# Sharing batch 3's expert sums between VectorE and GpSimd, and reordering the work around them, in an eight-layer transformer kernel

## The chip, the cores and the metric

The kernel runs on one core of a Trainium2 chip. The metric is the device time of one execution in microseconds (us). Engines are named as in the profile: PE is TensorE (PEld its weight loads), DVE VectorE, ACT ScalarE, POOL GpSimd, SP the engine that issues most transfers.

## The reference

The input x is 4 batches of 512 rows of 128 floats. Eight layers follow each other, four pairs of a cross-attention over 32 context rows and a feed-forward layer, each added to x after a layer norm:

```python
x = x + _L1_ffn_ref(_layernorm(x, axis=-1), ...)     # 16 experts, the best 3 of each row
x = x + _L2_xattn_ref(_layernorm(x, axis=-1), ...)   # 16 heads, softmax, causal mask

raw_gate = softmax(einsum('btd,de->bte', x, gate))
_, topk_idx = top_k(raw_gate, 3)                     # gates of the three, divided by their sum
hidden = relu(einsum('btd,edh->bteh', x, W1) + b1)
expert_out = einsum('bteh,ehd->bted', hidden, W2) + b2
return einsum('bte,bted->btd', gate_topk, expert_out)
```

The kernel numbers the layers 0 to 7. Layer 3 is the expert layer above, layer 4 the attention behind it. The change lies where layer 3 ends and layer 4 begins.

## The kernel before

x stays in on-chip memory as 16 tiles of 128 rows by 128 columns (tile t belongs to batch t // 4; W = 4 tiles of a batch, T = 16, S = 512, K = TOPK[3] = 3, D = P = 128). Each engine runs a list written out by hand and waits on semaphores. There is no scheduler.

Layer 3 scatters each row to the lists of its three experts in device memory. It then works through 63 slots of 128 rows: SP loads a slot, PE turns it (L2265), does the hidden product (L2273) and the second product (L2286, s_my), ACT does the relu (L1748), DVE adds the bias (L1321), and the rows are stored again. GpSimd gathers the finished rows back with indirect transfers (`gather`, L676, each one 128 rows): 12 for each batch, tile by tile and the three choices of a tile behind each other, three in flight. The first gather of a batch waits for the stores of its last slots (`PRIOR`); for batch 3 that is the last of the 63.

The three gathered rows of a row are weighted with gk and added to x. For batches 0 to 2 DVE does it (`add_experts`, L1308, 12 instructions a batch, four for each choice k). For batch 3 GpSimd does it (`add_last`): one product over all 12 tiles (L687) and three sums (L690). When a batch is summed, DVE takes its statistics (`stats_of`: L846, L849, L851, semaphore s_var), GpSimd the power of the variance (`power`: L630, L635, L637, s_rstd), ACT normalises the batch (`normed`, L1654), PE turns it (L2115, s_xT) and ACT copies the turned batch out of PSUM (`turned`, L1662). `power(n)` waits for the n-th statistics; powers 16 to 19 are those of batches 0 to 3 in layer 4, in this order.

Layer 4 runs in periods, one for each of the 16 tiles: PE computes the scores of tile t (L2127, s_s), DVE takes the maximum over each head and subtracts it (`max_sub`: L1252, L1256, and for the first tile of each batch the causal cap L1242), ACT takes the exponential, PE turns it (L2132) and multiplies with the values (L2143), DVE divides (`normalise`: L1265, L1269). `period(4, t)` of DVE holds `max_sub` of tile t + 1. Batches 1, 2 and 3 are normalised on ACT in its periods 0, 4 and 8 (`LATE`). In DVE's period 7 stands the wait for batch 3's sums (s_sum) and its statistics; until they are done DVE takes no further maximum. `add_bo` (L695) adds a bias to x on GpSimd after a batch was normalised.

Before the change DVE ends the expert layer with the last third of batch 1's sums and its statistics, and then starts period(4, -1), whose only work is the maximum of tile 0.

## Time and profile before

| | |
|---|---|
| median of 3 runs | 573.29 us (572.55 to 574.57) |
| the profiled execution's own time | 575.11 us |
| its span, first to last instruction | 573.4 us |
| granted PE clock, mean | 0.790 of full speed |
| busy share PE / PEld / DVE / ACT / POOL | 75% / 62% / 58% / 42% / 41% |

A row of the profile's timeline gives start and duration in us, engine, line, operation, output from input, and in brackets how long the engine sat idle before it and what ended that. The layer 3 to 4 boundary lies at 355 to 415 us of the span.

### The profile page before, as it was taken

What the parts mean: (1) busy time and instruction counts of PE and PEld (TensorE: products, weight loads), DVE (VectorE), ACT (ScalarE), POOL (GpSimd) and SP (SyncE); (2) the same over time, 40 slices, a digit from 0 to 9 for tenths busy, and PEclk for the clock granted to TensorE, in tenths of its full rate; (3) what the DMA queues carried; (4) which work ended last, traced back from release to release, by engine and by line L of the source; (5) the groups of instructions that cost most, each with busy time, mean ns of one, the idle gap of its engine ahead of it and who ended that gap; (6) DMA issues with size and microseconds to landing.
All of it is one profiled execution on the core that took longest, in us unless ns stands there. A gap on an engine that the chain in (4) does not pass through costs nothing.

```text
span 573.4 us, 9996 instructions
## 1 busy us (share of the span) xinstructions
PE 428.6 (75%) x2628; PEld 355.2 (62%) x2628; DVE 333.1 (58%) x1130; ACT 238.8 (42%) x635; POOL 234.8 (41%) x294
## 2 busy tenths in 40 slices
PE   5879678997898876529984749568899999982550
PEld 4768667995677775219973738436676667771440
DVE  6665355656786436215531317277776767858887
ACT  2332224664544212126752426334565646562221
POOL 2513730036327573720454341747811334533214
PEclk9795568999988557559995859778899999995555
DMA  6999546882651110212442323211000000000002
GB/s 188 299 403 388 122 123 212 290 284 54 203 187 46 34 48 16 80 37 70 130 117 61 98 60 89 74 32 39 0 1 2 1 0 1 2 1 1 0 1 73
DMA packets 60548, 55.42 MB, mean 97 GB/s; under 512 B 11922, under 2 KB 46446, under 8 KB 60366
## 3 DMA queue, kind: packets, MB, share of 16 engines
q1 hardware_dynamic: 53214, 43.64, 23.7%
q0 software_dynamic: 4736, 9.71, 5.8%
q10 hardware_dynamic: 2544, 1.44, 0.8%
q8 instruction: 23, 0.38, 0.3%
q14 instruction: 31, 0.25, 0.1%
HBM read 24.10 MB, written 30.67 MB: 96 GB/s over the span
## 4 chain that ended last, share of the span: by engine, by line
PE 44%; DVE 19%; another core or an unknown queue 9%; issue 9%; ACT 6%; POOL 5%; DVEq 5%; DMA 2%; SPq 2%; ACTq 0%; POOLq 0%
PE bank L2286 9%; PE bank L2273 8%; PE bank L2143 4%; PE bank L2127 3%; PE bank L2265 3%; PE bank L2132 2%; PE bank L2158 2%; PE bank L1982 2%; POOL wall L676 2%; DVE stats L846 2%; ACT xn L1654 2%; DVE e_sb L1256 1%; PE bank L2115 1%; PE bank L2416 1%
## 5 line engine op out<-in xcount | busy, mean ns | idle before, releaser
L1748 ACT ACTIVATE r<-bank,b 128x128 f32<-128x128 f32 x218 | 65.8, 365 | 56.1 <-PE bank L2273 33.8
L630 POOL TENSOR_TENSOR rstd<-veps,mhalf 128x4 f32<-128x4 f32 x32 | 33.8, 1056 | 132.0 <-DVE veps L851 131.6
L2286 PE MATMUL bank<-wall,r 128*128 x436 | 71.6, 299 | 20.9 <-ACT r L1748 17.6
L2286 PEld LDWEIGHTS bank<-wall,r 128*128 128x128 f32 x436 | 60.9, 207 | 23.9 <-issue 23.0
L2273 PE MATMUL bank<-on,e_sb 128*128 128x128 f32 x348 | 61.0, 310 | 9.0 <-issue 6.1
L676 POOL DMA_INDIRECT vZ<-outbuf,slots x40 | 39.2, 979 | 67.5 <-DMA outbuf<-h_sb 49.2
L1321 DVE TENSOR_TENSOR h_sb<-bank,b2all 128x128 f32<-128x128 f32 x86 | 25.0, 290 | 66.6 <-PE bank L2286 47.5
L2273 PEld LDWEIGHTS bank<-on,e_sb 128*128 128x128 f32 x348 | 51.5, 216 | 10.8 <-issue 10.8
L649 POOL DMA_INDIRECT outbuf<-h_sb,slots x48 | 46.5, 970 | 23.0 <-issue 15.1
L2143 PEld LDWEIGHTS bank<-vB,eT 128*128 128x128 f32 x384 | 52.7, 213 | 0.0
L2143 PE MATMUL bank<-vB,eT 128*128 128x36 f32 x384 | 52.5, 287 | 0.0
L1678 ACT COPY eT<-bank 128x512 f32<-128x512 f32 x48 | 28.0, 584 | 43.8 <-PE bank L2132 36.8
L1327 DVE COPY e_sb<-wall 128x256 f32 (+1 forms) x75 | 24.0, 323 | 36.4 <-PE bank L2273 23.2
L2265 PE MATMUL bank<-ident,h_sb 128*128 128x128 f32 x86 | 27.0, 316 | 20.3 <-issue 17.3
L1740 ACT COPY on<-bank 128x128 f32<-128x128 f32 x86 | 22.9, 267 | 44.4 <-PE bank L2265 22.8
L2127 PE MATMUL bank<-aB,xnT_all 128*128 128x512 f32 x64 | 36.0, 650 | 4.9 <-DVE e_sb L1256 4.0
L2132 PEld LDWEIGHTS bank<-ident,e_sb 128*128 128x128 f32 x192 | 25.9, 156 | 21.5 <-ACT e_sb L1674 9.9
L2132 PE MATMUL bank<-ident,e_sb 128*128 128x128 f32 x192 | 32.7, 298 | 2.4 <-ACT e_sb L1674 2.0
L846 DVE BATCH_NORM_STATS2 stats<-x 128x6 f32<-128x128 f32 x128 | 28.0, 281 | 5.3 <-POOL x L690 2.4
L2265 PEld LDWEIGHTS bank<-ident,h_sb 128*128 128x128 f32 x86 | 13.2, 154 | 26.7 <-issue 21.9
L2127 PE MATMUL bank<-VW,xnT_all 128*128 128x512 f32 x32 | 21.1, 752 | 8.5 <-ACT xnT_all L1662 5.0
L1654 ACT ACTIVATE xn<-x,nmr,rstd 128x128 f32<-128x128 f32 x48 | 19.7, 483 | 12.3 <-POOL nmr L637 12.3
(306 smaller groups left out, 876.3 us busy)
## 6 DMA issues: line engine op xcount, KB each, us to landing
outbuf<-zero SPq DMA_DIRECT2D x17, 1024.0 KB
wall<-in_w SPq DMA_DIRECT2D x4, 2048.0 KB, 13.8
outbuf<-h_sb SPq DMA_DIRECT2D x66, 64.0 KB
h_sb<-outbuf SPq DMA_DIRECT2D x63, 64.0 KB
h_sb<-rowbuf SPq DMA_DIRECT2D x23, 64.0 KB
outbuf<-h_sb POOLq DMA_DIRECT2D x20, 64.0 KB, 2.0
x<-in_x ACTq DMA_DIRECT2D x4, 256.0 KB, 6.3
b2all<-in_L_ffn_b SPq DMA_DIRECT2D x1, 1024.0 KB, 15.5
```

Source lines behind the costliest of these rows:

```text
L630: r = nc.gpsimd.tensor_tensor(rstd[:, at], veps[:, at], mhalf[:, 0:W], ALU.pow)
L649: i = nc.gpsimd.indirect_dma_start(rows_of[l][0:MOE[l][0] * REGION * P], bass.IndirectOffsetOnAxis(slots[:, k * T + t:k * T + t + 1], 0), ...
L676: nc.gpsimd.indirect_dma_start(tile_of(yg[l][b], w * K + k), None, outbuf[0:MOE[l][0] * REGION * P], bass.IndirectOffsetOnAxis(slots[:, c: ...
L846: v.bn_stats(stats[:, w * 6:w * 6 + 6], src(w))
L1654: i = a.activation(tile_of(dst, w), tile_of(x, b * W + w), ACT.Identity, bias=nmr[:, c:c + 1], scale=rstd[:, c:c + 1])
L1748: i = a.activation(hT[:, u * 512 + c * P:u * 512 + (c + 1) * P], bank[2 + u][:, c * P:(c + 1) * P], ACT.Relu, bias=b1[l][:, bass.ds(e * C ...
L2127: mm(s_ps[t % 2][:, :], tile_of(xnT_all, t), aB[l][:, (t // W) * 512:(t // W + 1) * 512], start=True, stop=True).then_inc(s_s, 1)
L2132: i = nc.tensor.transpose(tile_of(e_ps[t % 2], c), e_sb[:, (t % 2) * 512 + c * P:(t % 2) * 512 + (c + 1) * P], ident[:, :])
L2143: i = mm(o_ps[p % 2][:, at + c * VC:at + (c + 1) * VC], eT[:, (t % 2) * 512 + c * P:(t % 2) * 512 + (c + 1) * P], vB[l][:, ((t // W) * 4 + ...
L2265: nc.tensor.transpose(bank[4 + s % 2][:, 0:P], tile_of(xs, s % PLACES), ident[:, :]).then_inc(s_xt, 1)
L2273: h = mm(tile_of(bank[2 + s % 2], c), tile_of(w1s[l][s % RING], c), tile_of(xsT, s % 2), start=True, stop=True)
L2286: y = mm(bank[6 + s % 2][:, 0:P], hT[:, (s % 2) * 512 + c * P:(s % 2) * 512 + (c + 1) * P], wall[:, bass.ds(e * n + (WHALF + c * P), P)], ...
```

## The change

Four edits. (1) GpSimd's `add_last` leaves the first two tiles of batch 3 (`BY_VECTOR`) to DVE, which adds them in a new function `add_first` in period 5 of layer 4 after the first six gathers of batch 3. (2) GpSimd's power(17), batch 1's, stands behind nine gathers of batch 2 and ahead of its last three, where it stood behind all twelve. (3) DVE takes period(4, -1), the maximum of tile 0, ahead of the last third of batch 1's sums and of its statistics. (4) power(19), batch 3's, stands ahead of add_bo(1), where it stood behind it.

```diff
@@ -59,6 +59,7 @@
 ROUND = 1.5 * 2.0 ** 30
 RING = 4
 LATE = (0, 4, 8)
+BY_VECTOR = 2
 REGION = T + 1
 GRID = 16
 TAB = 4 * GRID + 1 + D
@@ -681,10 +682,11 @@
                 pool.wait_ge(s_gsub, 2)
                 for i in range(UNDER_WAY[3]):
                     pool.wait_ge(*gathered(3, last_of(3, 3) - i))
-                rows = yg[3][3][:, 0:W * K * D].rearrange("p (w k f) -> p w k f", w=W, k=K)
-                own = tile_of(x, 3, S).rearrange("p (w f) -> p w f", w=W)
-                weights = gk[:, :].rearrange("p (k t) -> p t k", k=K)[:, 3 * W:4 * W]
-                nc.gpsimd.tensor_tensor(rows, rows, weights.unsqueeze(3).to_broadcast([P, W, K, D]), ALU.mult).then_inc(s_sum, 1)
+                n = W - BY_VECTOR
+                rows = yg[3][3][:, BY_VECTOR * K * D:W * K * D].rearrange("p (w k f) -> p w k f", w=n, k=K)
+                own = x[:, (3 * W + BY_VECTOR) * P:4 * W * P].rearrange("p (w f) -> p w f", w=n)
+                weights = gk[:, :].rearrange("p (k t) -> p t k", k=K)[:, 3 * W + BY_VECTOR:4 * W]
+                nc.gpsimd.tensor_tensor(rows, rows, weights.unsqueeze(3).to_broadcast([P, n, K, D]), ALU.mult).then_inc(s_sum, 1)
                 for k in range(K):
                     pool.wait_ge(s_sum, k + 1)
                     nc.gpsimd.tensor_tensor(own, own, rows[:, :, k], ALU.add).then_inc(s_sum, 1)
@@ -741,15 +743,16 @@
             gather(3, 0)
             gather(3, 1)
             power(16)
-            gather(3, 2)
+            gather(3, 2, 0, 9)
             power(17)
+            gather(3, 2, 9)
             gather(3, 3, 0, 8)
             power(18)
             gather(3, 3, 8)
             add_last()
             add_bo(0)
+            power(19)
             add_bo(1)
-            power(19)
             add_bo(2)
             add_bo(3)
             for n in range(20, 24):
@@ -1281,6 +1284,8 @@
                 if l == 4 and t == 2:
                     add_experts(3, 2, (2,))
                     stats_of(norm_no(4, 2), 2)
+                if l == 4 and t == 5:
+                    add_first()
                 if l == 4 and t == 7:
                     dve.wait_ge(s_sum, TOPK[3] + 1)
                     stats_of(norm_no(4, 3), 3)
@@ -1308,6 +1313,19 @@
                             i = v.scalar_tensor_tensor(tile_of(x, t), tile_of(yg[3][b], w * K + k), gk[:, k * T + t:k * T + t + 1],
                                                        tile_of(x, t), ALU.mult, ALU.add)
                 i.then_inc(s_gad, 1)
+
+            def add_first():
+
+                K, first = TOPK[3], last_of(3, 2) + 1
+                for i in range(UNDER_WAY[3]):
+                    dve.wait_ge(*gathered(3, first + BY_VECTOR * K - 1 - i))
+                for k in range(K):
+                    if k:
+                        dve.drain()
+                    for w in range(BY_VECTOR):
+                        t = 3 * W + w
+                        v.scalar_tensor_tensor(tile_of(x, t), tile_of(yg[3][3], w * K + k), gk[:, k * T + t:k * T + t + 1],
+                                               tile_of(x, t), ALU.mult, ALU.add)
 
             def moe(l):
                 E, C = MOE[l]
@@ -1351,9 +1369,6 @@
                         add_experts(3, 1, ((s + 4 - NS) // 2,))
                 for s in range(NS - LAG, NS):
                     add_bias(s, experts[s])
-                if l == 3:
-                    add_experts(3, 1, (2,))
-                    stats_of(norm_no(4, 1), 1)
 
             def v_loads(src, E):
 
@@ -1430,7 +1445,10 @@
                     dve.wait_ge(s_r5, b * 4 + (c + 1))
                     v.tensor_tensor(tile_of(h_sb, (b % 2) * 4 + c, S), r, r, ALU.mult).then_inc(s_q5, 1)
 
-            for t in range(-1, 18):
+            period(4, -1)
+            add_experts(3, 1, (2,))
+            stats_of(norm_no(4, 1), 1)
+            for t in range(18):
                 period(4, t)
             squares(0)
             squares(1)
```

On VectorE, at the end of the expert layer, before (L1308 is `add_experts`, L846 to L851 the statistics, vZ the gathered rows of batches 1 and 2, gk the weights, and L1242 to L1256 `max_sub`):

```order
L1308 SCALAR_TENSOR_TENSOR x<-vZ,gk,x 128x128 [waits s_gat0,s_gat1,s_gat2]
L1308 SCALAR_TENSOR_TENSOR x<-vZ,gk,x 128x128 x3
L846 BN_STATS stats<-x 128x6 x4
L849 BN_AGGR mv<-stats 128x2 x4
L851 TENSOR_SCALAR veps<-mv 128x4
L1242 TENSOR_TENSOR bank<-bank,cap 32x512 [waits s_s]
L1252 TENSOR_REDUCE mx<-bank 128x16
L1256 TENSOR_TENSOR e_sb<-bank,mx 128x512
```

and in the changed kernel, where the same functions have the lines L1313, L849 to L854 and L1245 to L1259:

```order
L1245 TENSOR_TENSOR bank<-bank,cap 32x512 [waits s_s]
L1255 TENSOR_REDUCE mx<-bank 128x16
L1259 TENSOR_TENSOR e_sb<-bank,mx 128x512
L1313 SCALAR_TENSOR_TENSOR x<-vZ,gk,x 128x128 [waits s_gat0,s_gat1,s_gat2]
L1313 SCALAR_TENSOR_TENSOR x<-vZ,gk,x 128x128 x3
L849 BN_STATS stats<-x 128x6 x4
L852 BN_AGGR mv<-stats 128x2 x4
L854 TENSOR_SCALAR veps<-mv 128x4
```

The maximum of tile 0, with its wait for PE's scores (s_s), moved from behind batch 1's last sums and statistics to ahead of them.

On GpSimd, from the last gathers of batch 2 on, before (L630 is the power with its wait for the statistics, wall takes batch 3's rows, s_ys0 to s_ys7 are the stores that `PRIOR` names):

```order
L676 DMA vZ<-outbuf,slots 128x128 [waits s_gat1]
L676 DMA vZ<-outbuf,slots 128x128 [waits s_gat2]
L630 TENSOR_TENSOR rstd<-veps,mhalf 128x4 [waits s_var]
L635 TENSOR_SCALAR nmr<-mv 128x4
L637 TENSOR_TENSOR nmr<-nmr,rstd 128x4 [waits s_pw]
L676 DMA wall<-outbuf,slots 128x128 [waits s_ys4,s_ys3,s_ys5,s_ys2,s_ys6,s_ys1,s_gat0,s_ys0,s_ys7]
```

and in the changed kernel, where `gather` is L677 and `power` L631 to L638:

```order
L677 DMA vZ<-outbuf,slots 128x128 [waits s_gat2]
L631 TENSOR_TENSOR rstd<-veps,mhalf 128x4 [waits s_var]
L636 TENSOR_SCALAR nmr<-mv 128x4
L638 TENSOR_TENSOR nmr<-nmr,rstd 128x4 [waits s_pw]
L677 DMA vZ<-outbuf,slots 128x128 [waits s_gat0]
L677 DMA vZ<-outbuf,slots 128x128 [waits s_gat1]
L677 DMA vZ<-outbuf,slots 128x128 [waits s_gat2]
L677 DMA wall<-outbuf,slots 128x128 [waits s_ys4,s_ys3,s_ys5,s_ys2,s_ys6,s_ys1,s_gat0,s_ys0,s_ys7]
```

The power, and so its wait for batch 1's statistics, now stands ahead of three gathers of batch 2, and those are ahead of batch 3's first gather.

On VectorE in period 5 and 6 of layer 4 of the changed kernel (L1272 is the end of `normalise`, L1327 the new `add_first`):

```order
L1272 TENSOR_TENSOR on<-bank,rs 128x256
L1327 SCALAR_TENSOR_TENSOR x<-wall,gk,x 128x128 [waits s_gat0,s_gat1,s_gat2]
L1327 SCALAR_TENSOR_TENSOR x<-wall,gk,x 128x128 x5
L1255 TENSOR_REDUCE mx<-bank 128x16 [waits s_s]
L1259 TENSOR_TENSOR e_sb<-bank,mx 128x512 [waits s_e]
L1245 TENSOR_TENSOR bank<-bank,cap 32x512 [waits s_s]
```

The six new instructions stand between the division of tiles 2 and 3 and the maximum of tile 7; the wait for all of batch 3's sums stays behind the maximum of tile 8.

## Rows read from the trace of the kernel before

**Rows 1.** GpSimd's timeline, gathers of batches 2 (vZ) and 3 (wall).
```profile
357.65 1.21 POOL L676 DMA_INDIRECT vZ<-outbuf,slots  x1 [0.80 <-DMA outbuf<-h_sb]
...
368.24 0.94 POOL L676 DMA_INDIRECT vZ<-outbuf,slots  x1 [0.30 <-issue]
...
371.98 0.94 POOL L676 DMA_INDIRECT vZ<-outbuf,slots  x1 [0.30 <-issue]
378.59 1.05 POOL L630 TENSOR_TENSOR rstd<-veps,mhalf 128x4 f32<-128x4 f32 x1 [5.67 <-DVE veps L851]
...
379.96 0.20 POOL L637 TENSOR_TENSOR nmr<-nmr,rstd 128x4 f32<-128x4 f32 x1
380.95 1.07 POOL L676 DMA_INDIRECT wall<-outbuf,slots  x1 [0.80 <-issue]
...
392.52 1.07 POOL L676 DMA_INDIRECT wall<-outbuf,slots  x1 [0.16 <-issue]
...
396.40 0.94 POOL L676 DMA_INDIRECT wall<-outbuf,slots  x1 [0.30 <-issue]
399.07 2.78 POOL L687 TENSOR_TENSOR wall<-wall,gk 128x1536 f32<-128x1536 f32 x1 [1.72 <-DMA wall<-outbuf,slots]
401.93 3.97 POOL L690 TENSOR_TENSOR x<-x,wall 128x512 f32<-128x512 f32 x3
...
409.81 0.20 POOL L637 TENSOR_TENSOR nmr<-nmr,rstd 128x4 f32<-128x4 f32 x1
```

**Rows 2.** ScalarE's timeline, last relu and batch 0's turned copy.
```profile
369.35 0.62 ACT L1748 ACTIVATE r<-bank,b 128x128 f32<-128x128 f32 x2 [2.15 <-remote]
374.93 0.69 ACT L1662 ACTIVATE xnT_all<-bank,ones 128x512 f32<-128x512 f32 x1 [4.95 <-remote]
```

**Rows 3.** TensorE's timeline at the boundary and after batch 3's statistics.
```profile
367.26 1.11 PE L2115 MATMUL bank<-ident,xn 128*128 128x128 f32 x4 [0.56 <-issue]
...
375.67 3.78 PE L2127 MATMUL bank<-VW,xnT_all 128*128 128x512 f32 x4 [4.32 <-ACT xnT_all L1662]
...
409.79 1.30 PE L2127 MATMUL bank<-VW,xnT_all 128*128 128x512 f32 x2 [2.21 <-DVE e_sb L1256]
...
414.47 2.06 PE L2127 MATMUL bank<-VW,xnT_all 128*128 128x512 f32 x2
...
419.02 1.02 PE L2127 MATMUL bank<-VW,xnT_all 128*128 128x512 f32 x2
```

**Rows 4.** GpSimd's timeline, last of batch 0's twelve gathers.
```profile
308.18 0.94 POOL L676 DMA_INDIRECT h_sb<-outbuf,slots  x1 [0.30 <-issue]
```

**Rows 5.** VectorE's timeline, the bias add that follows that gather.
```profile
311.61 0.29 DVE L1321 TENSOR_TENSOR h_sb<-bank,b2all 128x128 f32<-128x128 f32 x1 [6.12 <-remote]
```

**Rows 6.** VectorE's timeline from the last slot to batch 3's statistics.
```profile
375.16 0.29 DVE L1321 TENSOR_TENSOR h_sb<-bank,b2all 128x128 f32<-128x128 f32 x1 [1.89 <-remote]
...
378.34 0.17 DVE L851 TENSOR_SCALAR veps<-mv 128x4 f32<-128x4 f32 x1
378.42 0.68 DVE L1242 TENSOR_TENSOR bank<-bank,cap 32x512 f32<-32x512 f32 x1
...
382.67 0.69 DVE L1256 TENSOR_TENSOR e_sb<-bank,mx 128x512 f32<-128x512 f32 x1
383.55 2.40 DVE L1308 SCALAR_TENSOR_TENSOR x<-vZ,gk,x 128x128 f32<-128x128 f32 x8 [0.19 <-DMA wall<-outbuf,slots]
...
400.65 0.69 DVE L1242 TENSOR_TENSOR bank<-bank,cap 32x512 f32<-32x512 f32 x1 [1.70 <-PE bank L2127]
...
403.20 0.42 DVE L1269 TENSOR_TENSOR on<-bank,rs 128x256 f32<-128x256 f32 x1
406.00 0.87 DVE L846 BATCH_NORM_STATS2 stats<-x 128x6 f32<-128x128 f32 x4 [2.37 <-POOL x L690]
```

**Rows 7.** Chain that ended last: start, length, engine, tile and line.
```profile
410.30 1.64 ACT xn L1654 x4
```

**Rows 8.** Busy time and PE clock in 410 to 415 us.
```profile
410.00:415.00 5.00, 4.95 (x19) 3.84 (x19) 4.54 (x16) 3.92 (x9) 3.91 (x6) 0.56 0.00 0
```

## The prediction

> **What bounds the kernel now.** I read the chain that ended last first, then the timelines of the five engines at the boundary of layers 3 and 4. In that chain batch 3 enters layer 4 at 410.30, when ScalarE normalises it [rows 7]. What let it start is the row of batch 3's statistics: VectorE had ended tiles 4 and 5's division at 403.62 and stood 2.37 us until GpSimd's last sum of batch 3 [rows 6]. So GpSimd's queue sets this place. Read backwards it is one unbroken run [rows 1]: sums and product 399.07 to 405.90, a wait for the last gather from 397.34, four gathers from 392.52, a power, eight gathers from 380.95, power(17) from 378.59. Ahead of power(17) GpSimd stood 5.67 us, waiting for VectorE's statistics of batch 1. VectorE wrote these at 378.34, right behind the last slot's bias add at 375.16 [rows 6].
>
> Why was the last slot so late? TensorE's record has batch 0's turn at 367.26 [rows 3], but ScalarE, whose relu ended at 369.97, could copy it only at 374.93 and stood 4.95 us on "remote" [rows 2]. GpSimd ended batch 2's twelfth gather at 372.92 [rows 1], 2.0 us before. Batch 0's run of twelve gathers ended at 309.12 [rows 4], and VectorE stood 6.12 us and got its product 2.5 us later, at 311.61 [rows 5]. Starts and ends of matmuls are modelled, the waits of the other two engines are not. I read: while GpSimd issues a long run of gathers, TensorE's results come late, and all are out 2.0 to 2.5 us after the run.
>
> **The change, part by part.** The sum runs from 372.92 on, against the profile's own execution (575.11 us, span 573.4); the difference is then put on the median, 573.29.
>
> *Nine gathers, then the power.* The ninth gather ends at 369.18 instead of the twelfth at 372.92 [rows 1], and GpSimd then only waits. With 2.0 to 2.5 us behind that, the turned batch 0 and the last two second products come at 371.2 to 371.7; I take 371.4, against 374.93. The bound on the other side is that TensorE's delay has nothing to do with the gathers: then 374.93 stays. I take the first, since both runs shown ended so. Gain here: 3.5 us, for the tail of the expert layer.
>
> *First maximum ahead of batch 1's last sums.* It needs the scores of tile 0: ScalarE's copy 0.69 [rows 2], then half of 3.78 for one of the two scores in that row [rows 3], so 371.4 + 0.7 + 0.05 + 1.9 = 374.1. VectorE has done the bias adds before this and waits some 2 us. The three maxima from 378.42 to 383.36 took 4.94 [rows 6]; without the 0.68 of the cap that is 1.4 each, and 2.1 for the first. It ends at 376.3. Behind it stand batch 1's sums and statistics, which took from 375.45 to 378.51, 3.06 us [rows 6]: 379.4. GpSimd starts power(17) at 379.5, which is 0.9 us later than 378.59. So the 3.5 us gained are spent: 2.3 on waiting for scores and 2.1 on the maximum, both now ahead of the statistics.
>
> *Three gathers behind the power.* The power takes 1.57 (378.59 to 380.16), the next gather starts 0.16 to 0.8 later, and gathers follow each other at 1.25, as the distance of the ninth from the twelfth shows (3.74 for three) [rows 1]. They used to lie under the 5.67 us wait; now they lie on the path, ahead of batch 3's first gather: 3.75 and 0.15 for one more start, 3.9 us. The eight, the power(18) and the four behind them are the same.
>
> *Half of the sums to VectorE.* GpSimd's product took 2.78 and three sums 3.97 [rows 1]. A tiny instruction on GpSimd takes 0.20 [rows 1], so of a half-size product and three half-size sums no more than that is fixed in each: 1.5 + 3 x 0.75 + gaps 0.2 = 3.9 against 6.83, a saving of 2.9; if nothing is fixed, 3.4. I take 3.1. If the time did not fall with size at all it would be 0.
>
> *add_first on VectorE.* Eight instructions of this form took 2.40 [rows 6], 0.30 each, while gathers ran. Six and three starts of 0.1 are 2.1 us. Their six gathers are done long before. The two columns of engines meet at batch 3's statistics, so VectorE's own arrival counts too. Before, it waited for no gather at 383.55. Now batch 2's last gather starts at 381.1 + 0.15 + 2.6 = 383.85, and lands 2.7 later, as 396.40 to 399.07 shows [rows 1]: 386.6. VectorE, done with three maxima at 382.3, stands some 4 us and goes on 3.0 us later than before. From there it needs the same 20.1 us to 403.62 [rows 6], plus 2.1, less pauses that a late engine doesn't have (1.70 at 400.65 [rows 6], less than 1 elsewhere): 406.3 to 408.7.
>
> *power(19) ahead of add_bo(1)* is worth nothing: that power ended at 410.01 [rows 1], just ahead of ScalarE's start at 410.30 [rows 7], and ScalarE was held by VectorE's next maximum. If ScalarE's order were not the limit it would be at most 1.3 us, the length of an add over a batch (a third of 3.97 [rows 1]), but then only beyond the 0.3 us that the power was early.
>
> Sum on GpSimd: + 0.9 + 3.9 - 3.1 = **+1.7 us**; batch 3's statistics start at 407.7 and not 406.0, inside VectorE's own 406.3 to 408.7. Everything behind follows batch 3 through the chain. Prediction: 573.29 + 1.7 = **575.0 us**. The profiled execution, 575.11, would be 576.8. 0.3% is 1.7 us, about what a measurement of this kernel can tell from no change; my forecast lies on that line.
>
> **A rule weighed against the trace.** ScalarE's 4.95 us on "remote", ended 2.0 us after the last gather [rows 1, 2], are what the gain of the nine gathers rests on. The Trainium skill ("SBUF — State Buffer", Who interferes with whom) says that TensorE and ScalarE never wait on anyone and that no DMA contends with a compute engine. By that rule the gathers would not hold TensorE, the sum would lack its 3.5 us, and it is a rival below. The rows speak against it twice, though they show a coincidence in time and no mechanism.
>
> **Rivals.**
> *A. The gathers don't hold TensorE* (by that rule). The turned batch comes at 374.93 as before, scores at 377.6, the maximum ends at 379.8, statistics at 382.9: power(17) 4.4 us late. Sum 4.4 + 3.9 - 3.1 = +5.2: 578.5. For it: nothing names the gather in ScalarE's wait. Against it: two runs ended alike. Chance 0.13.
> *B. The longer run starves layer 4.* Batch 3's gathers were eight and, after a power, four; now eleven follow each other. If TensorE falls silent for the last 6 us of a long run, as in [rows 5], to 2 us after the end at about 395.5, VectorE, which has three to five maxima to take there, stands 1 to 3 us and reaches the statistics at 409 to 410. +3 to +4: 576.8. Against it: VectorE has 2.4 + 1.1 us of sums and batch 2's statistics in that time. Chance 0.2.
> *C. The clock stays up.* Before, TensorE had stood 2.21 us until 409.79, and the granted clock is 0.56 in 410 to 415, so mostly the lower level, 1.2 GHz; a score took 2.06 at 414.47 and 1.02 at 419.02 [rows 3, 8]. With VectorE arriving nearly together with GpSimd, TensorE's pause shrinks by up to 2. If then the clock stays at 2.4 GHz through batch 3's turn, the path gets back 1.1 to 2.5 us: +0.6 to -0.8, 573.2; with the saving on the sums at 3.4 and the turned batch at 371.2, -1.3. It decides where the pause stays short enough, which no row tells. Chance 0.17.
> *D. Faster.* The same clock gain where, in addition, the first maximum finds its score earlier, because TensorE's last products come with the ninth gather and not 2 us after: another 2.0. -2 to -3: 570.9. It ends faster than before only if both hold. Chance 0.08.
> Forecast (+0.5 to +2.9, by the two arrivals): 0.42.
>
> **Numbers.** The range runs from C to A: 572.3 to 578.5. Slower by over 0.3% (over 575.0) takes half of the forecast, all of A and most of B and a little of them joined: 0.48. Faster by over 0.3% is D and the low end of C: 0.10. Same: 0.42.
>
> **What would show it.** In the changed profile ScalarE's copy of batch 0 should start near 371.4 (A: 374.9), the first cap at 374.1, power(17) at 379.5 with some 10 us idle ahead of it, batch 3's first gather at 385.7 against 380.95, VectorE standing about 4 us until 386.6 ahead of batch 2's sums, GpSimd's product at half of 2.78, and batch 3's statistics at 407.7. The prediction is wrong if power(17) starts before 378, if VectorE doesn't wait for batch 2's gathers, or if the chain no longer runs through batch 3's statistics.

## The result and the profile after

The changed kernel takes 577.4 us (median of 22 runs, 571.9 to 584.4), the kernel before 574.35 us beside it (22 runs). The ratio is 1.0117, with a 95% interval of 1.0083 to 1.0150: slower, where 575.0 and a ratio of 1.003 were forecast. The profiled execution took 579.72 us (span 578.0) against 575.11 (span 573.4), +4.6 us. Ratios leave out the runs more than 1.5% above the fastest of their kernel, medians hold all of them; by the medians alone the change costs 0.5%. So the direction is clear and the size is known only roughly.

GpSimd's timeline of the changed kernel, from batch 2's ninth gather on (start, us, engine, line, op, tiles, idle before and what ended it):

```profile
368.51 0.95 POOL L677 DMA_INDIRECT vZ<-outbuf,slots  x1 [0.30 <-issue]
379.22 1.05 POOL L631 TENSOR_TENSOR rstd<-veps,mhalf 128x4 f32<-128x4 f32 x1 [9.76 <-DVE veps L854]
...
380.94 1.07 POOL L677 DMA_INDIRECT vZ<-outbuf,slots  x1 [0.16 <-issue]
...
384.84 0.94 POOL L677 DMA_INDIRECT wall<-outbuf,slots  x1 [0.30 <-issue]
...
400.17 0.94 POOL L677 DMA_INDIRECT wall<-outbuf,slots  x1 [0.30 <-issue]
402.77 1.48 POOL L689 TENSOR_TENSOR wall<-wall,gk 128x768 f32<-128x768 f32 x1 [1.65 <-DMA wall<-outbuf,slots]
404.33 2.34 POOL L692 TENSOR_TENSOR x<-x,wall 128x256 f32<-128x256 f32 x3
406.63 1.32 POOL L697 TENSOR_TENSOR x<-x,bo 128x512 f32<-128x512 f32 x1
414.35 1.05 POOL L631 TENSOR_TENSOR rstd<-veps,mhalf 128x4 f32<-128x4 f32 x1 [6.41 <-DVE veps L854]
```

Beside [rows 1]: power(17) at 379.22 and not 378.59, batch 3's first gather at 384.84 and not 380.95, the product in 1.48 and not 2.78, and the sums done at 406.67 where they ended at 405.90. GpSimd is 0.8 us late, less than the 1.7 forecast. But power(19) then waits 6.41 us for VectorE: it is VectorE now, and not GpSimd, that sets when batch 3 goes on.

VectorE's timeline of the same kernel:

```profile
373.86 0.69 DVE L1245 TENSOR_TENSOR bank<-bank,cap 32x512 f32<-32x512 f32 x1 [1.76 <-PE bank L2145]
...
376.33 1.14 DVE L1313 SCALAR_TENSOR_TENSOR x<-vZ,gk,x 128x128 f32<-128x128 f32 x4 [0.26 <-issue]
...
386.09 2.35 DVE L1313 SCALAR_TENSOR_TENSOR x<-vZ,gk,x 128x128 f32<-128x128 f32 x8 [4.23 <-DMA vZ<-outbuf,slots]
...
399.35 0.69 DVE L1255 TENSOR_REDUCE mx<-bank 128x16 f32<-128x512 f32 x1 [2.19 <-remote]
...
402.28 0.36 DVE L1268 RECIPROCAL rs<-bank 128x32 f32<-128x32 f32 x1 [1.47 <-remote]
...
403.05 5.30 DVE L1327 SCALAR_TENSOR_TENSOR x<-wall,gk,x 128x128 f32<-128x128 f32 x6
...
412.70 0.87 DVE L849 BATCH_NORM_STATS2 stats<-x 128x6 f32<-128x128 f32 x4
```

Beside [rows 6]: the first maximum is where it was forecast (373.86 for 374.1), so is the wait for batch 2's last gather (until 386.09 for 386.6). From there VectorE needed 26.6 us to batch 3's statistics, where 383.55 to 403.62 was 20.1. They start at 412.70, 6.7 us later than 406.00. The six new adds take 5.30 us, not 2.1, and their row lies beside GpSimd's rows from 402.77 to 407.95. Ahead of them stand two pauses of 3.66 us together, in which VectorE waits for TensorE's results.

ScalarE's timeline of the same kernel, the turned copy of batch 0, a copy (`eT`) of turned exponentials in the middle of the stretch, and the normalisation of batch 3 behind its statistics:

```profile
371.01 0.69 ACT L1680 ACTIVATE xnT_all<-bank,ones 128x512 f32<-128x512 f32 x1 [0.78 <-remote]
...
396.47 0.59 ACT L1696 COPY eT<-bank 128x512 f32<-128x512 f32 x1 [6.00 <-remote]
...
417.11 1.64 ACT L1672 ACTIVATE xn<-x,nmr,rstd 128x128 f32<-128x128 f32 x4
```

The copy came at 371.01 for a forecast 371.4 and 374.93 before [rows 2]. At 396.47 ScalarE had stood 6.00 us for a result of TensorE, whose own record has it done at 392.86; that was 1.9 us behind the end of the run of eleven gathers (394.54); the longest stand of the kernel before in that stretch is 2.56 us. Batch 3 enters layer 4 at 417.11 and not 410.30 [rows 7], 6.8 us later; the whole span is 4.6 us longer, so 2.2 are given back behind it. The busy windows show where the clock was meanwhile (span; busy time and instructions of TensorE, its weight loads, VectorE, ScalarE, GpSimd; granted clock; DMA share and GB/s):

```profile
410.00:415.00 5.00, 5.00 (x23) 4.12 (x23) 4.46 (x16) 1.97 (x4) 0.65 (x1) 0.66 0.00 0
415.00:420.00 5.00, 4.45 (x32) 3.36 (x30) 4.68 (x14) 3.62 (x8) 4.45 (x6) 1.00 0.00 0
```

Before, the granted clock was 0.56 in 410 to 415 [rows 8], while batch 3's turn and its first scores were computed, and a score pair took 2.06 us [rows 3]. Now batch 3 comes to TensorE behind 415, where the clock is 1.00. TensorE's timeline:

```profile
409.77 1.31 PE L2145 MATMUL bank<-VW,xnT_all 128*128 128x512 f32 x2 [2.31 <-DVE e_sb L1259]
414.52 1.10 PE L2145 MATMUL bank<-VW,xnT_all 128*128 128x512 f32 x2
416.71 1.10 PE L2145 MATMUL bank<-VW,xnT_all 128*128 128x512 f32 x2
```

TensorE had stood 2.31 us until 409.77, as long as the 2.21 before [rows 3], and the clock was 0.66 behind it too, but that stretch was over when batch 3 came. The second power behind power(19), power(21), stands at 428.67 against 423.88, +4.8, and the difference changes little from there to the end (+4.6).

### The profile page after: what moved, and what is told of

It reads as the page before. It is cut to its first block, busy times and chain, and to the rows that moved or that the text cites. A ratio compares the mean times of both kernels' runs of the same rounds, so it can differ in the third digit from the quotient of the medians.

```text
span 578.0 us, 10005 instructions
## 1 busy us (share of the span) xinstructions
PE 432.5 (75%) x2628; PEld 357.2 (62%) x2628; DVE 336.9 (58%) x1136; ACT 239.5 (41%) x635; POOL 232.9 (40%) x294
## 4 chain that ended last, share of the span: by engine, by line
PE 42%; DVE 21%; another core or an unknown queue 12%; issue 6%; ACT 6%; DVEq 5%; DMA 2%; POOL 2%; SPq 2%; ACTq 0%; POOLq 0%
PE bank L2304 9%; PE bank L2291 8%; PE bank L2145 4%; PE bank L2161 3%; PE bank L2283 2%; PE bank L2150 2%; DVE e_sb L1259 2%; PE bank L2000 2%; ACT xn L1672 2%; PE bank L2176 2%; DVE stats L849 2%; PE bank L2133 1%; PE bank L2434 1%; DMA b2all<-in_L_xattn_Wv 1%
## 5 line engine op out<-in xcount | busy, mean ns | idle before, releaser
L631 POOL TENSOR_TENSOR rstd<-veps,mhalf 128x4 f32<-128x4 f32 x32 | 33.8, 1057 | 142.0 <-DVE veps L854 141.7
L677 POOL DMA_INDIRECT vZ<-outbuf,slots x40 | 39.0, 974 | 65.1 <-DMA outbuf<-h_sb 48.1
L2291 PE MATMUL bank<-on,e_sb 128*128 128x128 f32 x348 | 59.5, 304 | 5.7 <-issue 4.1
L2291 PEld LDWEIGHTS bank<-on,e_sb 128*128 128x128 f32 x348 | 50.0, 211 | 7.7 <-issue 7.5
L2150 PEld LDWEIGHTS bank<-ident,e_sb 128*128 128x128 f32 x192 | 27.5, 163 | 24.9 <-ACT e_sb L1692 11.4
L2283 PE MATMUL bank<-ident,h_sb 128*128 128x128 f32 x86 | 26.6, 312 | 21.4 <-issue 18.2
L2150 PE MATMUL bank<-ident,e_sb 128*128 128x128 f32 x192 | 34.6, 310 | 3.6 <-ACT e_sb L1692 3.5
L849 DVE BATCH_NORM_STATS2 stats<-x 128x6 f32<-128x128 f32 x128 | 28.0, 281 | 3.0
L2145 PE MATMUL bank<-VW,xnT_all 128*128 128x512 f32 x32 | 24.2, 855 | 5.5 <-DVE e_sb L1259 5.4
L1682 ACT COPY xnT_all<-bank 128x512 f32<-128x512 f32 x24 | 14.0, 583 | 27.1 <-PE bank L2133 26.4
```

The source lines that it names most:

```text
L631: r = nc.gpsimd.tensor_tensor(rstd[:, at], veps[:, at], mhalf[:, 0:W], ALU.pow)
L677: nc.gpsimd.indirect_dma_start(tile_of(yg[l][b], w * K + k), None, outbuf[0:MOE[l][0] * REGION * P], bass.IndirectOffsetOnAxis(slots[:, c: ...
L849: v.bn_stats(stats[:, w * 6:w * 6 + 6], src(w))
L2145: mm(s_ps[t % 2][:, :], tile_of(xnT_all, t), aB[l][:, (t // W) * 512:(t // W + 1) * 512], start=True, stop=True).then_inc(s_s, 1)
L2150: i = nc.tensor.transpose(tile_of(e_ps[t % 2], c), e_sb[:, (t % 2) * 512 + c * P:(t % 2) * 512 + (c + 1) * P], ident[:, :])
L2283: nc.tensor.transpose(bank[4 + s % 2][:, 0:P], tile_of(xs, s % PLACES), ident[:, :]).then_inc(s_xt, 1)
```

## The experiments

There were eighteen runs, some of the same kernel on another chip, in five groups, each group on one chip and beside the kernel before. The chips fall into two kinds by their times. On three of the five (the second, fourth and fifth group) the kernel before takes 573 to 577 us, as where the prediction was made; these are the first kind below. On two (the first and third group) the same kernel takes 511 us; these are the second kind. A ratio is always against the kernel before on the same chip.

### One edit at a time, where gathers delay nothing (before: 511.61 us)

The change has four edits: (1) the sums shared, (2) nine gathers ahead of power(17), (3) the first maximum moved, (4) power(19) ahead of add_bo(1). The sharing alone is the diff's `add_last`, `add_first` and its call; e2_nine_only is this alone:

```
-            gather(3, 2)
+            gather(3, 2, 0, 9)
             power(17)
+            gather(3, 2, 9)
```

e4_no_share has edits 2, 3 and 4, e5_no_max has 1, 2 and 4.

> Edit 1 alone (two tiles of batch 3's sums to VectorE in period 5), the rest as before. Theory P (port): in the changed kernel add_first's six instructions took 5.3 us and not 2.1 because they ran at the same time as GpSimd's product and sums, both reading on-chip memory. Alone, add_first should begin near 397, where GpSimd still issues gathers, and end about when GpSimd's product begins (399.1): 2.1 us, less than 1 us of overlap. GpSimd's sums end at 403.0, batch 3's statistics start at 403.6 to 405 against 406.0: 1 to 2.4 us faster than before. Theory F (form): the six are slow for themselves (their rows lie in another tile than before), then 5.3 us here too, VectorE arrives at 407: 1 us slower.

> Edit 2 alone: power(17) behind nine gathers of batch 2, statistics of batch 1 still ahead of the first maximum. Theory G (gathers hold TensorE): ScalarE's copy of batch 0 at 371.0 as in the changed kernel, batch 1's statistics at 375.2, power(17) at 375.3, batch 3's first gather at 381.0 as before. GpSimd's sums still end at 405.9, so within 0.5 us of before, unless theory R (a run of eleven gathers starves TensorE for its last 4 to 6 us and VectorE stands) costs more than the 2.4 us that VectorE has spare: then up to 1.5 us slower. Rival N (gathers don't hold TensorE): copy at 374.9, first gather of batch 3 at 384.8, 3.9 us slower.

> Edits 2, 3 and 4 without the sharing. GpSimd's sums start at 402.8 as in the changed kernel and take 6.8: 409.6. Theories P and R: VectorE, without add_first, arrives at 403.1 + 3.9 = 407.0 and waits; batch 3's statistics at 409.6, 3.1 us ahead of the changed kernel's 412.7 and 3.6 behind before. The two pauses of together 3.7 us in VectorE (399 and 402) stay, since they come from the run of gathers. If instead the sharing caused them, VectorE arrives at 403.3.

> Edits 1, 2 and 4 without the first maximum moved. Batch 1's statistics end at 375.2, power(17) at 375.3, batch 3's first gather at 381.0, batch 2's sums can start at 382.3. Theory R: pauses of some 3 to 4 us stay in VectorE, because eleven gathers still follow each other; VectorE comes to add_first at 399.3, by theory P on top of GpSimd's product (399.1 to 403): 5 us, statistics at 408 to 409, 2 to 3 us slower than before. Without R and P: add_first at 396, statistics at 404, 2 us faster than before.

Measured: e1 0.9906 (0.9866 to 0.9946), e2 0.9982 (0.9944 to 1.0020), e4 0.9993 (0.9961 to 1.0024), e5 0.9899 (0.9861 to 0.9938). On this chip ScalarE never stood for the turned batch. Its timeline in e1_share_only:

```profile
303.38 0.61 ACT L1765 ACTIVATE r<-bank,b 128x128 f32<-128x128 f32 x2
304.23 0.69 ACT L1679 ACTIVATE xnT_all<-bank,ones 128x512 f32<-128x512 f32 x1 [0.24 <-PE bank L2132]
```

0.24 us, where [rows 2] has 4.95. VectorE's timeline of the same kernel has the six adds long ahead of GpSimd's product (333.63), and the wait at batch 3's statistics is still GpSimd's:

```profile
327.59 1.98 DVE L1326 SCALAR_TENSOR_TENSOR x<-wall,gk,x 128x128 f32<-128x128 f32 x6
...
337.62 0.87 DVE L848 BATCH_NORM_STATS2 stats<-x 128x6 f32<-128x128 f32 x4 [3.33 <-POOL x L692]
```

So the six adds cost 2.0 us by themselves, within the 2.1 of the prediction's price, and the sharing is worth 1% where VectorE has slack. The form of the instruction is not what made them dear. The expectations of this group are in the times of the first kind, and two of them missed: e5 was to be 2 to 3 us slower and is 1.0% faster, e4 was to be late by 3.6 us at batch 3 and takes the time of the kernel before.

### One edit at a time, first kind (before: 577.32 us)

e3_max_only has edit 3 alone. e6_share_late is the changed kernel, and e7_nine_share_late the changed kernel without edit 3, both with add_first behind the wait for GpSimd's sums. e8_gathers_after_tail is the kernel before, where GpSimd starts batch 2's gathers only when batch 0 has been turned:

```
# e6, e7
                 if l == 4 and t == 7:
                     dve.wait_ge(s_sum, TOPK[3] + 1)
+                    add_first()
# e8
+            pool.wait_ge(s_xT, norm_no(4, 0) + 1)
             gather(3, 2)
             power(17)
```

> Edit 3 alone: the first maximum ahead of batch 1's last sums, twelve gathers ahead of the power as before. ScalarE's copy stays at 374.9 (theory G), the first maximum ends at 379.8, batch 1's statistics at 382.9, power(17) 4.4 us later than before. All of GpSimd's chain moves by that: batch 3's statistics at 410.3, 4.4 us slower than before. A rival by which GpSimd's queue isn't what sets this place: under 1 us slower.

> The changed kernel, but add_first stands behind the wait for GpSimd's sums in period 7 and so can't run beside them (only beside add_bo(0)). Theory P: the six take 2.1 us, at most 3.4 with add_bo's 1.3 in the way; VectorE arrives at 407.0, batch 3's statistics at 409.2 to 410.4 against 412.7: 2.3 to 3.5 us faster than the changed kernel. Theory F: 5.3 us there too, statistics at 412.3.

> Edits 1, 2 and 4, statistics of batch 1 ahead of the first maximum as before, add_first behind the wait for GpSimd's sums. GpSimd's sums end at 403.0. With theory R's pauses VectorE arrives at 403.2, add_first 2.1 to 3.4 us: statistics at 405.4 to 406.6, within 0.6 us of before. Without the pauses it arrives at 400 and waits: statistics at 405.1 to 406, 0 to 0.9 us faster than before.

> Before, but GpSimd's first gather of batch 2 waits until TensorE has turned batch 0 of layer 4, so no gather runs beside the last slots. Theory G: with no gathers in that stretch TensorE's results come promptly, ScalarE's copy of batch 0 at about 364 to 367 against 374.9. Rival N: the delay has another cause, and the copy stays near 374.9. The time: the gathers start some 8 us later, GpSimd's chain is late by 1 to 3 us at batch 3's first gather, and now twenty gathers run on layer 4's first tiles: 1 to 5 us slower than before.

Measured: e3 1.0042 (1.0013 to 1.0070), e6 1.0055 (1.0019 to 1.0091), e7 1.0037 (0.9998 to 1.0075), e8 0.9994 (0.9965 to 1.0024). ScalarE's timeline of e8_gathers_after_tail, and GpSimd's first gather of batch 2 behind it:

```profile
366.80 0.61 ACT L1749 ACTIVATE r<-bank,b 128x128 f32<-128x128 f32 x2
367.65 0.69 ACT L1663 ACTIVATE xnT_all<-bank,ones 128x512 f32<-128x512 f32 x1 [0.24 <-PE bank L2116]
```

```profile
367.90 1.07 POOL L676 DMA_INDIRECT vZ<-outbuf,slots  x1 [7.89 <-PE bank L2116]
```

Without gathers in that stretch the copy is held for 0.24 us and not 4.95. It comes 9.3 us behind power(16), where the kernel before has 19.7 (power(16) at 358.35 here, 355.20 there). That settles the premise of the nine gathers and ends rival A for this kind of chip: with the gathers there TensorE's results are late, without them they are not. Whether it is GpSimd's issuing or the transfers themselves, no run separates. The kernel is no faster: the gathers themselves now lie on the path, and power(17) comes 24.5 us behind power(16) for 23.4 before.

e3 shows edit 3 as a cost by itself: 4.8 us at batch 3's statistics, where 4.4 were expected, but only 0.4%, 2.4 us by the medians, in the time. In e6 and e7, where the six adds start after GpSimd's rows have ended, they took 1.98 us each time; but there they lie whole behind the wait they were meant to shorten, and neither gains anything. Both missed what was expected of batch 3's statistics. e7 has them 1.5 us later than the kernel before behind power(16) (52.3 for 50.8), where at most 0.6 was expected. e6 has them at 59.0, where 2.3 to 3.5 us less than the changed kernel's 57.2 was expected; its traced execution took 588.63 us, 6.7 over its median, and VectorE stood 7.6 us for TensorE in it.

### The changed kernel's parts again (before: 510.75 us)

e9_changed_again is the changed kernel. e10_first_at_3 is this with one number changed, e11_no_max_at_3 takes edit 3 back in addition, e12_share_again is e1:

```
-                if l == 4 and t == 5:
+                if l == 4 and t == 3:
                     add_first()
```

> The changed kernel once more, beside the three below. Two kinds of chip are known by now: one on which the kernel before takes some 577 us and ScalarE's copy of the turned batch 0 waits 5 us during gathers, and one on which it takes some 512 us and that copy waits for nothing. On the first kind: ratio 1.005 to 1.015, add_first 5.0 to 5.6 us for six instructions beside GpSimd's product and sums. On the second kind the changed kernel has not run; the gathers don't hold TensorE there and VectorE reaches its period 5 during gathers (327 to 330 us, as in the runs with the sharing), so add_first should take 2.0 us; the sharing without the first maximum gave 0.990, the first maximum with nine gathers and no sharing 0.999. Theory of the collision: 0.990 to 0.997. If add_first is dear by its own form, it takes 5.3 us there too.

> The changed kernel with add_first two periods earlier (behind tile 4's maximum), nothing else moved: no row of GpSimd's product and sums is near it, only gathers and a power. Theory of the collision: 2.0 us for the six instead of 5.3; VectorE's arrival at batch 3's statistics falls from 6.7 us later than before by 3.3, and by more where the early adds fill VectorE's pauses of 2.2 and 1.5 us: 407.4 to 409.4 in the time scale of the changed kernel's profile (after its batch 2 sums at 386.1: 21.3 to 23.3 us from their start to batch 3's statistics, where the changed kernel has 26.6). Time 0.993 to 0.997 of the changed kernel on a chip of the first kind, so 1.000 to 1.008 of the kernel before; the same as the changed kernel within 0.3% on one of the second kind. Rival, the price is of the instruction: six still take over 4 us and the time stays that of the changed kernel.

> As the one above, and the first maximum back behind batch 1's last sums and statistics. The first maximum alone made the kernel 0.4% slower, by its wait for a score and 2.1 us of its own ahead of power(17). Expected: power(17) 3.5 to 5 us earlier against power(16) than in the kernel with the maximum first, batch 3's statistics 2 to 4 us earlier than there; 0.990 to 0.998 of the kernel before on a chip of the first kind, 0.988 to 0.994 on one of the second. Rival, that the pauses for TensorE give any earlier start back: equal to the run above within 0.3%.

> The sharing of batch 3's sums alone, in the place of the change (period 5), once more. On a chip of the second kind it gave 0.991 with add_first at 1.98 us. On one of the first kind VectorE's period 5 lies near 400 us and GpSimd's product starts near 399 in the kernel before, so the two should run beside each other: add_first 4.5 to 5.5 us, GpSimd's sums done 3 us earlier than before but VectorE not, batch 3's statistics -0.5 to +2.5 us: 0.999 to 1.005. Rival, no collision: 2.0 us and 0.993 to 0.997.

Measured: e9 0.9952 (0.9919 to 0.9986), e10 0.9976 (0.9949 to 1.0004), e11 0.9915 (0.9881 to 0.9949), e12 0.9868 (0.9814 to 0.9923). This chip was of the second kind again. VectorE's timeline of e9_changed_again:

```profile
321.70 2.35 DVE L1313 SCALAR_TENSOR_TENSOR x<-vZ,gk,x 128x128 f32<-128x128 f32 x8 [4.28 <-DMA vZ<-outbuf,slots]
...
334.77 2.01 DVE L1327 SCALAR_TENSOR_TENSOR x<-wall,gk,x 128x128 f32<-128x128 f32 x6
...
342.46 0.87 DVE L849 BATCH_NORM_STATS2 stats<-x 128x6 f32<-128x128 f32 x4 [1.42 <-POOL x L692]
```

The same program that is 1.2% slower on one chip is 0.5% faster on this one. From batch 2's sums to batch 3's statistics VectorE needs 20.8 us with no pause for scores but 1.42 for GpSimd, against 26.6. Its six adds end at 336.78, ahead of the product at 338.46, and cost 2.01. Without the first maximum (e11) power(17) comes 13.8 us behind power(16) and not 16.5 as in e10 (2.7 earlier, where 3.5 to 5 were expected of a chip of the first kind), batch 3's statistics 4.2 us earlier behind power(16) (42.4 for 46.5), the kernel takes 0.6% less than e10, and the sharing alone is best. The two places of add_first are alike in time within the error, as expected where there is nothing to meet.

### The place of the six adds, first kind (before: 572.95 us)

e13_changed_third is the changed kernel, e14_first_at_3_again is e10, e15_first_at_7 has add_first two periods later, ahead of the wait for GpSimd's sum, and e16_share_third is e1.

> The changed kernel a third time, for the pair with the next. On a chip of the first kind (the kernel before some 575 us) 1.005 to 1.015 and add_first 5 to 5.6 us; on one of the second kind (some 511 us) 0.992 to 0.999 and 2.0 us.

> The changed kernel with add_first two periods earlier; it has run on a chip of the second kind alone, where there was nothing to collide with in either place, and the two were alike within the error. On a chip of the first kind, theory of the collision: add_first 2.0 us and 0.993 to 0.997 of the changed kernel's time. Theory that the place of batch 3's statistics is held by the pauses for TensorE: add_first 2.0 us, but the pauses grow by as much, and the time stays within 0.3% of the changed kernel. On one of the second kind: alike within 0.4%.

> The changed kernel with add_first two periods later, right ahead of VectorE's wait for GpSimd's last sum. On a chip of the second kind VectorE came there at 341.0 us, and GpSimd's sums and its add over a batch lay from 340.0 to 343.6: part of the six now run beside them. Collision: 3 to 4.5 us for six, against 2.0 in the middle of gathers, on the same chip; the statistics 2 to 3 us later than in the changed kernel, 1.003 to 1.008 of its time. If VectorE's price has nothing to do with GpSimd: 2.0 us again. On a chip of the first kind VectorE comes there 2 us after GpSimd's adds have ended: 2.0 us, and 0.994 to 0.998 of the changed kernel.

> The sharing alone, in period 5. On a chip of the first kind, collision: add_first 4 to 5.5 us and 0.999 to 1.005 of the kernel before; no collision: 2.0 us, 0.993 to 0.997. On one of the second kind: 0.987 to 0.991 as twice before.

Measured: e13 1.0003 (0.9962 to 1.0043), e14 0.9998 (0.9957 to 1.0039), e15 1.0086 (1.0051 to 1.0121), e16 0.9985 (0.9946 to 1.0024). The six adds took 5.20 us in e13, 1.98 in e14, 2.11 in e15 and 1.99 in e16. In e15 they started 0.3 us ahead of the end of GpSimd's last add (408.74 for 1.27 us), VectorE's timeline:

```profile
409.69 2.11 DVE L1326 SCALAR_TENSOR_TENSOR x<-wall,gk,x 128x128 f32<-128x128 f32 x6
411.88 0.87 DVE L849 BATCH_NORM_STATS2 stats<-x 128x6 f32<-128x128 f32 x4
```

My expectation for e16 missed: VectorE stood for no score there and came to period 5 at 396.87, 2.0 us ahead of GpSimd's product, so nothing met. e15 missed too: its batch 3's statistics came 2.1 us earlier behind power(16) than e13's (55.3 against 57.4), and yet it took 0.4% longer by the medians; what took that back I don't know. The traces show nothing that did: the traced execution of e15 took 578.27 us and that of e13 580.79, which is 5.5 over e13's median, so the two traced executions stand the other way round than the medians. e14 missed as well: 0.993 to 0.997 of the changed kernel was expected, and it took 0.999 of it by the medians, though its batch 3's statistics came 2.7 us earlier behind power(16) (54.7). And e13 missed by its ratio: the changed kernel cost nothing measurable by it, although its medians stand +0.4% apart (575.33 against 572.95), near the +0.5% of the first measurement. The price in time of the collision stayed open.

### The meeting forced, and the adds moved away, first kind (before: 572.96 us)

e17_meet makes add_first wait for the same gathers as GpSimd's product (the wait is on the last three), so that both start together. e18_first_at_3_third is e10 once more.

```
-                    dve.wait_ge(*gathered(3, first + BY_VECTOR * K - 1 - i))
+                    dve.wait_ge(*gathered(3, last_of(3, 3) - i))
```

> The changed kernel, but VectorE's add_first waits for the same gathers as GpSimd's product (the last four of batch 3), so that both start together on any chip. On a chip of the first kind that is what the changed kernel does anyway: 5.2 to 5.3 us for six, statistics of batch 3 some 26.5 us after the start of batch 2's sums. On one of the second kind the six took 2.0 us alone (334.8, with the product at 338.5): collision now 5.3 us there too, starting with the product, and VectorE comes to the statistics some 5 us later than in the changed kernel, 1.007 to 1.012 of its time, or 1.002 to 1.007 of the kernel before. Without a collision: 2.0 us, and only the wait of 3.7 us is added.

> The other half of the pair: the changed kernel with add_first in period 3, 2.0 us, no meeting on either kind. If the collision is worth its 3.2 us in the time: 0.992 to 0.996 of the run above on a chip of the first kind, and 0.988 to 0.994 on one of the second. If the pauses for scores give it back: within 0.3% of it on the first kind.

Measured: e17 1.0097 (1.0051 to 1.0142), e18 1.0014 (0.9976 to 1.0051), medians 577.57 and 573.83; e18 stands at 0.992 of e17 by the ratios, 0.9935 by the medians. VectorE's timeline of e17_meet:

```profile
401.42 5.52 DVE L1327 SCALAR_TENSOR_TENSOR x<-wall,gk,x 128x128 f32<-128x128 f32 x6 [2.85 <-DMA wall<-outbuf,slots]
...
411.29 0.87 DVE L849 BATCH_NORM_STATS2 stats<-x 128x6 f32<-128x128 f32 x4
```

and GpSimd's:

```profile
401.52 1.59 POOL L689 TENSOR_TENSOR wall<-wall,gk 128x768 f32<-128x768 f32 x1 [1.80 <-DMA wall<-outbuf,slots]
403.19 2.34 POOL L692 TENSOR_TENSOR x<-x,wall 128x256 f32<-128x256 f32 x3
405.48 1.31 POOL L697 TENSOR_TENSOR x<-x,bo 128x512 f32<-128x512 f32 x1
```

VectorE's timeline of e18_first_at_3_third:

```profile
395.41 1.98 DVE L1327 SCALAR_TENSOR_TENSOR x<-wall,gk,x 128x128 f32<-128x128 f32 x6
...
405.65 0.69 DVE L1245 TENSOR_TENSOR bank<-bank,cap 32x512 f32<-32x512 f32 x1 [2.18 <-PE bank L2145]
...
408.75 0.87 DVE L849 BATCH_NORM_STATS2 stats<-x 128x6 f32<-128x128 f32 x4
```

The two kernels have the same instructions, in another place and with another wait, and e18 needs 22.9 us from batch 2's sums (385.83) to batch 3's statistics, e17 27.1 (from 384.23). Starting 0.1 us ahead of the product, the six adds take 5.52 us and end with GpSimd's last row; beside gathers they take 1.98. GpSimd loses 0.1 us on its product and nothing on the sums. The pair is not the collision alone: e17 stands 2.85 us for gathers that e18 doesn't wait for, and e18 stands longer for scores. All the pauses together are 3.7 us in e17 and 3.2 in e18, so of the 4.1 us between them 3.5 are the adds and 0.5 the waits. The Trainium skill ("SBUF — State Buffer", Who interferes with whom) says that a VectorE instruction with two inputs in SBUF, the on-chip memory, contends with a GpSimd instruction that reads SBUF; add_first reads a gathered tile and x, both in SBUF. The traces agree, also in what they spare: VectorE's cap of the scores, with one input in PSUM (`bank`) and 0.69 us long at 405.65, lies beside GpSimd's last sum (404.19 to 406.52 in e18) and costs what it always costs.

## Why the prediction was wrong

The measured median, 577.4 us, lies inside the range that was given, 572.3 to 578.5. That is luck: the upper end was put there for rival A, which did not happen. Two terms of VectorE's column failed, the price of add_first and the pauses ahead of it; GpSimd's column, on which the sum was built, was 0.9 us off.

The columns are worked out from the traces as the rows above and [rows 1, 6] are, though not every row of them is shown; power(16) is at 355.20 before, 355.46 after, 357.34 in e3, 357.01 in e7, 354.40 in e16, 353.58 in e17 and 354.95 in e18. All are of the first kind.

```
kernel                        power(16) to power(17)  power(16) to batch 3's statistics
before                        23.4                    50.8
e3   first maximum alone      28.1                    55.6
e7   nine gathers, adds late  19.5                    52.3
e16  sharing alone            23.4                    48.8
changed                       23.8                    57.2
e17  changed, adds meet       23.8                    57.7
e18  changed, adds at 3       24.0                    53.8
```

*The path to power(17): right, part by part.* Nine gathers gained 3.9 us where 3.5 were forecast, the first maximum cost 4.7 where 4.4 were, and together they left +0.4 (forecast +0.9). The premise, that gathers hold TensorE, was shown by e8. The rule of the Trainium skill that was weighed against it ("SBUF — State Buffer", Who interferes with whom) does not fit what was measured on this kind of chip, a copy held 4.95 us beside gathers and 0.24 without them; it fits the second kind, 0.24 beside gathers.

*Three gathers on the path, half the sums: right, with small misses.* GpSimd's sums ended 0.8 us later, where +1.7 was forecast. power(17) was 0.6 us late for 0.9. The three gathers cost 3.3 us and not 3.9: from power(17) to batch 3's first gather it was 5.62 us against 2.36, since the gap behind the power fell from 0.80 to 0.16. The saving was 2.9 for 3.1 (1.48 + 2.34 and gaps against 2.78 + 3.97, that is 3.9 us for 6.8).

*add_first: the step that failed.* "Six and three starts of 0.1 are 2.1 us" took its price from adds that ran beside gathers [rows 6] and used it beside GpSimd's product and sums. It was 5.30: +3.2. The two columns were costed apart, and nothing was put in for the one place where the same change has them run side by side.

*VectorE's arrival, "less pauses that a late engine doesn't have": the second miss.* Without the collision (e18) VectorE needed 22.9 us from batch 2's sums to the statistics. 20.1 and 1.98 leave +0.8, where the range 406.3 to 408.7 takes off 0.1 to 2.5. The pauses don't shrink with lateness: 3.2 us in e18 (0.43, 0.60, 2.18), 3.7 in the changed kernel, 2.4 before (with 0.72 that the rows shown leave out). This is 0.9 to 3.3 us. Put on the changed kernel's power(16), e18's 53.8 gives 409.3; with the collision it was 412.7. So even without the collision VectorE would have come behind GpSimd's sums and past the range, and its column set the place.

*Rivals.* A fell with e8, for this kind of chip, and D fell.

B was nearer than its chance of 0.2. It put VectorE at 409 to 410, and that is where it comes once the collision is out (409.3). Its reading, that TensorE's results stay away for the last 6 us of a long run of gathers to 2 us behind it, is what ScalarE's row at 396.47 shows (6.00 us, 1.9 behind the run). In the other traces of the first kind with a run of eleven ScalarE had a stand of 3.0 to 6.8 us as well (e6, e7, e13, e14, e15, e18), though it ended anywhere from 0.2 to 6.5 us behind the run, and only e17 had none. But the length of the run is not the whole cause: e3 has the old runs of eight and four, a stand of 3.79 us and pauses of 4.0 us (0.59, 0.57, 1.00, 1.83), while e16 has the same runs, no such stand and no pause for TensorE at all. TensorE's clock goes with the pauses too, though loosely. From batch 2's sums to batch 3's statistics the granted clock was 0.92 before and 0.99 in e16, but 0.69 in the changed kernel, 0.78 in e18 and 0.80 in e3 (and 0.86 in e15, with 3.8 us of pauses). On the second kind, without such stands, e10 had a clock of 0.69 and a pause of 3.33 us, e9 0.92 and none. Whether the low clock makes the pauses or the pauses the low clock, no run separates; it stays open what decides how long VectorE stands.

C's gain is there, 2.2 us, but by another way (TensorE's pause didn't shrink; batch 3 came after the slow stretch) and on top of a much larger loss; that the clock makes up all of the 2.2 us was read, not tried. C's own lowest sum, -1.3, is 572.0 and not the 572.3 at which the range begins; nothing hangs on it.

*From 6.8 us to the time.* The changed kernel's profile is 4.6 us longer: 6.8 late at batch 3, less 2.2 given back behind it. e17 against e18, 3.9 us apart in the second column, is 3.7 us by the medians, with e17's wait for gathers in it. The pair in which only the place of the adds differs, e14 against e13, showed the same 5.20 and 1.98 us in the traces, 2.7 us in the second column, and only 0.1% by the medians; executions of one kernel spread over 2% here, and the two groups don't agree within it. So the size of the instruction's price is shown three times (5.20, 5.30 and 5.52 us where the adds lie beside GpSimd's product and sums, 1.98 to 2.05 in the eleven runs where they don't), and its worth in time is not settled.

*The best version.* The sharing alone won on the second kind (0.991, 0.987) and is even on the first (0.9985, with 1 in the interval). Edit 3 is on the losing side of every comparison, 0.4% (e3) and 0.2% (e6 against e7) on the first kind, 0.1% (e4 against e2, which differ by edit 4 too) and 0.6% (e11 against e10) on the second; of these only e3 has an interval of its own that stands clear of 1. It should be taken back.

## What to carry over

When a sum is split over VectorE and GpSimd, price the parts as if they met, and look where they lie: an add with both inputs in SBUF took 0.33 us beside gathers and 0.9 beside GpSimd's arithmetic. Moving six such adds by two periods, one number in the code, took 3.2 us off them, though the time of the whole kernel hardly showed it (0.1%). A saving on the engine that waits last is worth only the distance to the next engine, so its arrival has to be costed as carefully, pauses included; and a pause seen once is to be carried forward whole unless its cause is known. And a trace is one execution: where executions spread over 2%, a few microseconds at one place of two traces say nothing yet of the two times.

## What was not expected of the hardware

The same program takes 511 us on two chips and 573 to 577 us on others. Where a run of GpSimd's gathers is under way, TensorE's results come up to 5 us late on the slower kind (ScalarE's copy 4.95 us held, 0.24 without the gathers) and on time on the faster (0.24 with them). The change had both signs: 1.0117 on one chip of the first kind, 1.0003 on another, 0.9952 on the one of the second kind where it ran.

The traces tell one difference between the kinds. The chain that ended last holds "another core or an unknown queue", the releaser that the timelines call "remote", for 7 to 12% of the span in every trace of the first kind (9% before, some 50 us of the 60 that lie between the kinds) and has no such entry in any of the second; and the mean granted clock is 0.78 to 0.81 against 0.83 to 0.86. What lies behind that no row tells, nor whether it belongs to the chip or to its state at the time, since each group had its own chip and ran once.
